# A fused pre-norm attention and ternary FFN kernel on Trainium2: reordering the start, with the FFN weights brought into chunk 0, the attention values placed behind all queries and keys, and the third chunk's norm and the first value groups moved back

## The reference, cut to what matters

```python
# x: (4, 2048, 256) float32, 16 heads of 16, sliding causal window of 64
def attn(h, Wq, Wk, Wv, Wo):
    q, k, v = (proj(h, W) for W in (Wq, Wk, Wv))            # einsum('bsd,ed->bse'), split in heads
    scores = einsum('bhqd,bhkd->bhqk', q, k) / 4 + bias      # bias: -inf outside the window
    return einsum('bsd,ed->bse', merge(softmax(scores) @ v), Wo)

def ffn(x, W1, b1, W2, b2):
    def quantize(W):                                         # ternary: -1, 0, 1
        return clip(round(W / (mean(abs(W)) + 1e-5)), -1, 1)
    h = relu(einsum('bsd,fd->bsf', x, quantize(W1)) + b1)    # 256 -> 1024
    return einsum('bsf,df->bsd' , h, quantize(W2)) + b2      # 1024 -> 256

x = x + attn(layernorm(x), Wq, Wk, Wv, Wo)
x = x + ffn(layernorm(x), W1, b1, W2, b2)
```

## Time and profile before

| what | us |
|---|---|
| median of 3 runs | 751.86 |
| the three runs | 755.77, 751.86, 751.81 |
| profiled execution, its own time | 754.12 |
| span of its profile | 752.3 |
| PE / ACT / DVE / POOL busy in it | 691.5 / 667.0 / 629.5 / 579.6 |

### The profile page before, as it was taken

How to read it: one execution, slowest core, us unless ns; L and a number is a source line. 1 busy time by engine, 2 the same in 40 slices (tenths; PEclk the granted TensorE clock), 3 DMA queues, 4 the chain that set the end, 5 groups by cost and what they waited for, 6 DMA issues and landing times.

```text
span 752.3 us, 25171 instructions
## 1 busy us (share of the span) xinstructions
PE 691.5 (92%) x8412; PEld 595.2 (79%) x8412; DVE 629.5 (84%) x1584; ACT 667.0 (89%) x2724; POOL 579.6 (77%) x788
## 2 busy tenths in 40 slices
PE   5545678999999999999999999999999999998888
PEld 4424567889888888888888888888888988887767
DVE  4354888898989989898989899898989888987844
ACT  4385859999999999999999999999999999997823
POOL 8063868879797888888897979888888978788820
PEclk9867869999999999999999999999999999999999
DMA  4495723436354544455363635554563536351000
GB/s 136 79 195 89 96 44 30 71 86 74 81 74 88 73 98 72 74 98 80 86 77 79 92 70 72 99 72 72 98 82 66 73 73 71 67 75 31 17 29 29
DMA packets 430777, 57.70 MB, mean 77 GB/s; under 512 B 403380, under 2 KB 422198, under 8 KB 430648
## 3 DMA queue, kind: packets, MB, share of 16 engines
q1 hardware_dynamic: 416072, 44.15, 40.0%
q10 hardware_dynamic: 14576, 11.93, 5.6%
HBM read 12.00 MB, written 8.39 MB: 27 GB/s over the span
## 4 chain that ended last, share of the span: by engine, by line
PE 71%; ACT 10%; POOL 6%; DVE 4%; issue 4%; SPq 3%; DMA 1%; ACTq 1%; POOLq 0%; DVEq 0%
PE ps L956 12%; PE ps L944 11%; PE ps L861 10%; PE ps L841 9%; PE ps L893 8%; PE ps L919 6%; ACT p L419 5%; PE ps L904 5%; SPq L237 3%; PE ps L939 3%; PE ps L836 3%; POOL tl L347 2%; POOL p L323 2%; PE ps L931 2%; PE ps L884 1%
## 5 line engine op out<-in xcount | busy, mean ns | idle before, releaser
L419 ACT ACTIVATE p<-ps,negm 128x96 f32<-128x96 f32 x1024 | 341.2, 375 | 14.6 <-DVE negm L620 11.2
L347 POOL TENSOR_TENSOR tl<-pt,th 128x384 f16<-128x384 f32 x256 | 235.4, 920 | 82.6 <-ACT th L428 74.4
L419 ACT ACTIVATION_READ_ACCUMULATOR p<-ps,negm 128x1 f32 x1024 | 247.8, 242 | 0.0
L323 POOL TENSOR_TENSOR p<-p,rden 128x384 f32<-128x384 f32 x256 | 211.5, 826 | 34.6 <-DVE rden L627 34.6
L633 DVE STREAM_TRANSPOSE pt<-p 128x384 f32<-128x384 f32 x256 | 141.8, 554 | 21.9 <-POOL p L323 21.6
L620 DVE TENSOR_REDUCE negm<-ps 128x4 f32<-128x384 f32 x256 | 133.5, 522 | 18.1 <-PE ps L841 17.1
L841 PE MATMUL ps<-k,qbd 128*128 128x96 f16 x2048 | 132.2, 209 | 0.0
L841 PEld LDWEIGHTS ps<-k,qbd 128*128 128x128 f16 x2048 | 118.6, 100 | 11.9 <-issue 0.3
L861 PE MATMUL ps<-th,vb 128*128 128x96 f16 (+1 forms) x1120 | 102.4, 207 | 5.6 <-POOL tl L347 5.6
L861 PEld LDWEIGHTS ps<-th,vb 128*128 128x128 f16 x1120 | 96.8, 101 | 6.7 <-POOL tl L347 6.6
L861 PE MATMUL ps<-tl,vb 128*128 128x96 f16 (+1 forms) x1120 | 101.6, 206 | 0.0
(11 more groups left out here) (115 smaller groups left out, 1434.1 us busy)
## 6 DMA issues: line engine op xcount, KB each, us to landing
k<-kst SPq DMA_DIRECT2D x60, 288.0 KB, 4.0
vb<-vd SPq DMA_DIRECT2D x256, 32.0 KB, 2.5
out<-x SPq DMA_DIRECT2D x32, 256.0 KB, 2.2
qbd<-qs SPq DMA_DIRECT2D x248, 32.0 KB, 2.2
x<-in_L_attn_hidden ACTq DMA_DIRECT2D x15, 512.0 KB, 4.6
vb<-in_L_ffn_W ACTq DMA_DIRECT2D x2, 1024.0 KB, 8.1
k<-kst ACTq DMA_DIRECT2D x4, 288.0 KB, 5.0
x<-in_L_attn_hidden ACTq DMA_DIRECT2D x1, 256.0 KB, 3.7
```

The source lines that it names most:

```text
L323: e.tensor_tensor(p3, p3, rden[n % 4][:, :].unsqueeze(2).to_broadcast([128, 4, 96]), ALU.mult).then_inc(s_nm, 1)
L347: e.tensor_tensor(tl[g % 2][:, o], pt[n % 3][:, :], th[g % 2][:, o], ALU.subtract).then_inc(s_lo, 1)
L419: ins = e.activation(p[:, 96 * u:96 * u + 96], bank[:, 96 * u:96 * u + 96], ACT.Exp, bias=m[:, u:u + 1], accum_out=r[:, u:u + 1])
```

## The change

SP issues the loads of W1 and W2 itself, ahead of its loop, and no longer ACT in slot 2. x of chunk 2 is loaded in slot -16, behind the weights' evacuation; x of chunks 3, 4 and 5 in slots 3, 9 and 15 (before: 7, 11, 15). The magnitudes are summed in slots -4, -3, 1 and 3 (before: 8 to 11), and everything ternary moves nine slots forward: sum in 4, thresholds in 6, comparisons in 7 to 14 (before 16 to 23). The low half of the biases moves from slot 5 to 0, and DVE's constants from slot -32 to -44.

Chunk 0 is placed in another order. t = 0: SP (heads 0, 1) and ACT (heads 2, 3, and the keys) in slot -8, before in -5 and -4. t = 1: all by SP, queries in slot -1 and keys in slot 0; before, half of the queries by SP in slot 4, half of them and the keys by ACT in slot 5. Values of chunk 0: SP in slot 1, now behind all of these; before in slot 0, ahead of the queries of t = 1.

Chunk 2's statistics, rstd and norm come seven slots later (1, 4 and 10; before -6, -3 and 3). The first group of attention values, its copy and its addition come two slots later (10, 11, 12; before 8, 9, 10). Banks 6 and 7 are dealt out from slot 15 on.

```diff
+W_ABS, W_TERNARY = (-4, -3, 1, 3), 6
+def norm_at(n, pos):
+    c = stage_a(n, pos)
+    return 2 if stage_a(n - 7, pos) == 2 else None if c == 2 else c
+def spread(n, pos, soonest):
+    c = stage_a(n, pos)
+    return 0 if n == soonest - 16 else c or None
+def values_at(n, lag):
+    return 0 if n == lag + 2 else group_at(n, lag) or None
...
-        nxt = nxt + 1 if slot >= 24 else (nxt + 1) % 2
+        nxt = nxt + 1 if slot >= W_TERNARY + 9 else (nxt + 1) % 2
...
+            e.dma_start(n1, w1_d.rearrange("(t p) d -> p t d", p=128)).then_inc(d_w["1"], 16)
+            e.dma_start(n2, w2_d.rearrange("(t p) f -> p t f", p=128)).then_inc(d_w["2"], 16)
             for n in SLOTS:
                 for t in range(2):
-                    c = stage_a(n, Q_DMA[t])
-                    if c is not None:
-                        place_q(e, c, t, range(4) if c else range(2))
-                    c = stage_a(n, K_DMA[t])
-                    if c is not None and c >= 1:
+                    c = spread(n, Q_DMA[t], A_Q[t] + 2)
+                    if c is not None:
+                        place_q(e, c, t, range(2) if n < -1 else range(4))
+                    c = spread(n, K_DMA[t], A_K[t] + 2)
+                    if c is not None and (c, t) != (0, 0):
                         place_k(e, c, t)
-                c = stage_a(n, V_DMA if n > 1 else V_DMA + 2)
+                c = spread(n, V_DMA, 17)
...
-                c = stage_a(n, A_RSTD)
+                c = norm_at(n, A_RSTD)
...
                 if n == -16:
                     weights(range(6))
+                    e.wait_ge(s_wlo, 4)
+                    load_x(2)
...
-                for t in range(2):
-                    if stage_a(n, Q_DMA[t] + 1) == 0:
-                        place_q(e, 0, t, range(2, 4))
-                        place_k(e, 0, t)
-                if n == -1:
+                if n == A_K[0] + 2 - 16:
+                    place_q(e, 0, 0, range(2, 4))
+                    place_k(e, 0, 0)
+                if n in (3, 9, 15):
                     e.wait_ge(s_wlo, 8)
-                    load_x(2)
-                if n == 2:
-                    load_ffn()
-                if n in (7, 11, 15):
-                    load_x((n + 5) // 4)
-                if 8 <= n < 12:
-                    magnitudes(n - 8)
+                    load_x((n + 15) // 6)
+                if n in W_ABS:
+                    magnitudes(W_ABS.index(n))
...
-                gg = group_at(n, PV_LAG + 1)
+                gg = values_at(n, PV_LAG + 1)
...
-                    c = stage_a(n, A_NORM[u])
+                    c = norm_at(n, A_NORM[u])
...
-                if n == -32:
+                if n == SLOTS[0]:
                     consts()
...
-                if n == 5:
+                if n == 0:
                     bias_low()
-                if n == 13:
+                if n == W_TERNARY - 2:
                     sums()
-                if n == 15:
+                if n == W_TERNARY:
                     thresholds()
-                if 16 <= n < 24:
-                    ternary(n - 16)
+                if 0 <= n - 1 - W_TERNARY < 8:
+                    ternary(n - 1 - W_TERNARY)
...
-                gg = group_at(n, O_ADD)
+                gg = values_at(n, O_ADD)
...
-                    c = stage_a(n, A_STATS[u])
+                    c = norm_at(n, A_STATS[u])
...
-                if n == 14:
-                    e.wait_ge(s_const, 2)
+                if n == W_TERNARY - 1:
                     mean()
-                if 15 <= n < 23:
-                    ternary(n - 15)
+                if W_TERNARY <= n < W_TERNARY + 8:
+                    ternary(n - W_TERNARY)
...
-                gg = group_at(n, PV_LAG)
+                gg = values_at(n, PV_LAG)
```

More of the change, by code:

```diff
@@ L385, in load_x @@
                 e.dma_start(xs[c % NX][:, :, :], x_t[c]).then_inc(d_x[c % NX], 16)
-            def load_ffn():
-                e.dma_start(n1, w1_d.rearrange("(t p) d -> p t d", p=128)).then_inc(d_w["1"], 16)
-                e.dma_start(n2, w2_d.rearrange("(t p) f -> p t f", p=128)).then_inc(d_w["2"], 16)
             def masks():
```

## The result

The changed kernel takes 735.75 us in the median of 4 runs (735.59 to 735.89). The kernel before, run beside it, takes 753.82 us (751.81 to 756.05, 4 runs). The ratio is 0.976, with a 95% interval of 0.9722 to 0.9797. The profiled execution took 735.64 us, its span is 733.8 us, 18.5 us shorter than before.

What follows compares the result with a forecast made beforehand. PE bounds the untouched middle, so time was sought in the start's stalls: 5.5 + 9.6 + 2.6 + 1.2 - 2.1 - 2.7 - 0.8 + 2.5 = 15.8 us, from a median of 751.86 to 736; range 731 to 744.

Steps and rivals of the forecast that it cites:

- To the first maximum: Start up to slot 0's maximum on DVE: 30.1 instead of 35.6, 5.5 us gained, bounds 3.0 and 6.5.
- The stall before slot 8: PE's wait for the t = 1 queries: the 9.58 us gap goes whole, 9.6 us gained, lower bound 8.
- The 2.6 us of ACT's issue: Slot 5: ACT no longer issues its half of the t = 1 placing, 2.6 us gained.
- the 1.2 of the biases: Slot 5: the biases' low half no longer holds DVE there, 1.2 us gained, between 0 and 1.8.
- The ternary slots: Moved from slots 16 to 23 to 7 to 14: 7.2 us lost there, about 4.5 gained by leaving, balance 2.7 lost.
- 0.8 of values(1): Slot 12: PE's values(1) waits for group 0's addition in the same slot, 0.8 us lost once, bounds 0 and 2.
- the bank wait: Slot 23: wo(0, 0) avoids the bank held by slot 22's queries, 2.5 us gained, bounds 1 and 3.
- The values' cover of 1 to 3 us: Slot 10: values issued in 13.01 us, landed by 50 to 51, wanted by values(0) near 52.
- the rival of the late values: Value DMAs again take 23.07 us, slot 10 waits some 8 us: gain 8, 743.9 us; chance 0.12.
- The clock at the start: Rival: projections at 1.2 GHz after PE's pause, about 3.5 us back, 739.6 us; chance 0.14.
- The end follows slot 24: Whatever brings slot 24 forward brings the end forward as much; slot 24's maximum at 95.1 instead of 110.94.
- Giving SP all query DMAs: SP's queue, t = 1 placing: all eight query DMAs cost 2.6 us of issue in slots 0 to 7, nothing else.

Runs made afterwards that it cites:

- e4: The changed kernel with DVE's constants in slot -32 again, behind the first statistics: 738.65 us.
- e1: The changed kernel with chunk 0's values placed by SP in slot -2, ahead of the queries and keys of t = 1: 739.79 us.
- e6: e5 with the two FFN weight loads also issued by ACT in slot 2 again, beside the placing of chunk 0: 743.57 us.
- e5: The changed kernel with all ternary work, magnitudes included, in its old slots and banks 6 and 7 from slot 24; FFN weights still loaded by SP: 738.22 us.
- e2: The changed kernel with banks 6 and 7 dealt out only from slot 24: 737.73 us.
- c0_after: The changed kernel itself, run once more as the yardstick: 736.27 us, ratio 0.9759.
- e8: The changed kernel with chunk 2's statistics and biases' low half in slot -7, its rstd in -3, magnitudes in 0 to 3, chunk 3's x in -3, statistics in 5: 730.88 us.
- e10: e8 with all eight query DMAs of t = 0 on SP and the magnitudes in slots 0, 0, 1 and 3: 731.81 us.
- e9_fill: The changed kernel with four unused matmuls behind the scores in each of slots 3 to 9: 736.09 us.
- e3_values8: The changed kernel with the first group of attention values, its copy and its addition in slots 8, 9, 10 again: 739.22 us.

## Why the prediction was right, point by point

The forecast of 736 us rested on a sum of 15.8 us; the two profiled executions differ by 18.5, and the medians of runs made side by side by 18.1. That the time came out almost exact is luck: the gain was forecast 2.3 us too small, and the median that I started from, 751.86, was 2 us below that of the run beside the changed kernel, at the low end of what the kernel before shows (751.3 to 756.7 over all runs). The mechanism held, one term was mis-sized. (The upper bounds of the terms add up to 20.4, not 19.5.)

*To the first maximum: right.* 5.5 us forecast, 5.54 measured; its start, the constants, 2.0 forecast and 2.5 at the transposes, 2.3 at slot 0 (e4). The 2 MB were hidden as said.

*The stall before slot 8: right in mechanism.* 9.6 + 2.6 + 1.2 - 2.1, less the first ternary slot, 0.9 of the 7.2, is 10.4 forecast for slots 0 to 8; 27.39 - 17.82 = 9.6 measured. Two causes shared the stall, as the prediction had them: the order of the queue (4.3 at slot 8 with the loads away, e1) and the loads beside the placing (5.0, e6 against e5). The 2.6 us of ACT's issue and the 1.2 of the biases were not tested by themselves.

*The ternary slots: mis-sized.* The prediction lost 2.7 us by the move and won 2.5 back by the banks. Measured, the move costs or gains less than 1 us (-0.3 to 0.9 gained, e5) and the banks 1.6 in their slot (e2). The term that failed is the 7.2 us put down as lost in the new slots. The stretch of slots 8 to 15 became longer by 4.1 us (4.9 in c0_after), not by the 7.1 that the sum had for it (6.3 of ternary work and 0.8 of values(1)). What the slots need after the change was right, 3.2 us each forecast and 23.20 / 7 = 3.3 measured. What they took before was not: the 2.3 to 2.4 us that the prediction takes from the trace are 19.12 / 7 = 2.7. That is a typical slot of this stretch and not its mean: slots 10, 13 and 14 took 3.57, 2.82 and 3.45 us, and DVE had idle time in the stretch that its new work could fill. The earlier trace rows show only slots 16 and 17. The windows of slots 8 to 15, before and after (the third busy time is DVE's):

```profile
63.00:82.12 19.12, 14.17 (x187) 11.64 (x185) 13.78 (x40) 16.91 (x72) 11.67 (x15) 0.95 0.55 99
```

```profile
47.89:71.09 23.20, 17.96 (x196) 14.71 (x193) 21.13 (x49) 17.15 (x71) 13.18 (x17) 0.78 0.51 75
```

DVE works 7.4 us more, but it was idle for 5.3 us before and for 2.1 after (1.7 of them the wait at the low clock before slot 11), so the stretch grew by 4.1. Leaving slots 16 to 23 and the bank wait gained 6.85 us, where 4.5 + 2.5 had been forecast.

*The values' cover of 1 to 3 us: wrong.* Their issue took 16.1 us and not 13.0, and the cover was gone by 1.02 us. This is the rival of the late values in small: forecast at 8 us for a full stretch, it cost 1. The prediction counted x of chunk 3 beside them and left out x of chunk 4; with the first moved away the issue took 14.5 (e8), with both 12.7 (e10).

*The clock at the start.* The sum was right for the profiled execution: 1.00 through the projections, though PE idled 2.17 us for Wq. But the rival exists: in one execution (e9_fill) the clock was at 0.50, 1.2 GHz, from 15 to 18 us, and slot 0 came 1.4 us later, not 3.5, as it rose again during the projections. In the other eleven executions with the constants first it stayed at 1.00 through them. From 12 to 15 us PE was busy 1.26 us in e9_fill and 1.30 in the changed kernel, so what it did before does not tell the two apart. The Trainium skill (TensorE: Matmul & The Clock Gate, section "The HAM clock gate") says that the throttled state is the default and that activity releases it. The traces agree in so far as the clock was at 1.00 after the early matmuls and fell, once in twelve, after a stretch with little work.

*The end follows slot 24: right.* 17.9 us at slot 24, 18.5 from slot 29 to 247, 18.5 at slot 255.

*Giving SP all query DMAs.* For t = 1 it cost nothing that shows: there is no wait for them, since they are wanted 14 us later. For t = 0 slot 0 came 3.5 us later (e10 against e8, which differ in two magnitude sums too, but PE's wait names the queries), as they are wanted at once. The Trainium skill (DMA: Bandwidth & Descriptors, section "Issuing engines are not separate DMA queues") says that issuing from several engines saves only the time of issue. The traces agree in part: of the 3.5 us, four more issues on SP at 0.69 are 2.75, and the DMAs, issued later and beside other transfers, also landed more slowly (4.0 us against 2.1 to 2.2). Here both were on the path.

What stays open: the two terms of 2.6 and 1.2 us, why e8's lead shrinks before slot 8, and whether unused matmuls on PE can hold the clock through slots 11 to 13. What the low clock costs is known only where two traces can be compared: 1.8 us in slot 10 (changed kernel against e2_banks24) and 1.6 in slot 12 (the other way round).

## What to carry to other kernels

A queue that serves several consumers should be ordered by when each is wanted, and a bulk load belongs where the DMA engines are idle, not where the queue seems free: each was worth 4 to 5 us here. Follow one instruction that every step has through all steps: it shows where a lead is won, given back and won again, while medians blur 1 to 3 us. Do it for two executions of the same kernel too, since the table has its own scatter. When work is moved into a stretch, cost it against that stretch's own idle time, not as if the engine were full there.

## What the runs showed of the hardware that I had not expected

Runs of one kernel on one chip differ by up to 5.1 us (the kernel before, seven runs beside c0_after: 751.61 to 756.68). Those of e8_better, 728.43, 728.88, 732.88 and 733.05, differ by 4.6, and in these four the time goes with the mean granted clock (0.984, 0.984, 0.979, 0.977). It does not in all: in e3_values8 the slowest run, 740.55 us, has the highest clock, 0.979. One place of it shows in the windows near the end, the changed kernel first, then e2_banks24, the same work, 1.2 us later:

```profile
670.00:680.00 10.00, 10.00 (x125) 9.04 (x122) 7.83 (x23) 8.43 (x42) 7.20 (x11) 0.83 0.01 2
```

```profile
671.20:681.20 10.00, 9.70 (x151) 9.00 (x150) 8.70 (x25) 9.95 (x47) 8.73 (x13) 1.00 0.01 2
```

In the ten microseconds before, PE was busy 7.4 us in both. In one execution the granted clock then fell, to 0.83 in the mean of the ten, in the other it did not, and e2_banks24, 1.2 us behind until slot 247, was 0.3 us ahead at slot 255. A kernel with short lulls on PE can thus have a time with several values. I also had not expected that the DMA issues on ACT cost as much as 3.9 us of its time for six transfers (3.05 for four query DMAs, 0.76 each, where SP needs 0.69).
